# Three cross attention layers: where the head sums are fetched, normalised and projected, and where the next loads are issued

## The reference

```
def _perceiver_layer(x, inp, Wq, bq, Wk, bk, Wv, bv, Wo, bo, W1, b1, W2, b2):   # layer 1
    q = (x @ Wq + bq).reshape(b, t, NUM_HEADS, HEAD_DIM)
    k = (inp @ Wk + bk).reshape(b, s, NUM_HEADS, HEAD_DIM)
    v = (inp @ Wv + bv).reshape(b, s, NUM_HEADS, HEAD_DIM)
    attn = softmax(einsum('bthd,bshd->bhts', q, k) / sqrt(HEAD_DIM))
    out = einsum('bhts,bshd->bthd', attn, v).reshape(b, t, DIM)
    x = x + (out @ Wo + bo)
    h = gelu(x @ W1 + b1)
    return x + (h @ W2 + b2)
```

## Time and profile before

| | |
|---|---|
| median of 3 runs | 4184.68 us (4180.75 to 4191.73) |
| the profiled execution, its own time | 4188.51 us |
| span of its trace | 4186.7 us |
| PE busy | 3623.1 us (87%) |
| DVE busy | 3421.4 us (82%) |
| ACT busy | 2804.7 us (67%) |
| mean granted TensorE clock | 0.911 |

### The profile page before, as it was taken

How to read it: one execution, slowest core, us unless ns; L and a number is a source line. 1 busy time by engine, 2 the same in 40 slices (tenths; PEclk the granted TensorE clock), 3 DMA queues, 4 the chain that set the end, 5 groups by cost and what they waited for, 6 DMA issues and landing times. The chain is left out here.

```text
span 4186.7 us, 85443 instructions
## 1 busy us (share of the span) xinstructions
PE 3623.1 (87%) x35126; PEld 1223.7 (29%) x35126; DVE 3421.4 (82%) x3310; ACT 2804.7 (67%) x4037; POOL 229.1 (5%) x196
## 2 busy tenths in 40 slices
PE   5676899999999848999999997199959999999995
PEld 2352322222222212222222222045522222222221
DVE  4333899999999548999999994399969999999972
ACT  0332388888888715888888886145517888888884
POOL 3000000000000000000000000234400000000000
PEclk9657699999999967999999999599958999999998
DMA  3102011111010130111111102300011111111100
GB/s 102 48 1 55 12 28 21 22 28 27 14 28 16 53 67 13 28 28 23 19 28 28 19 11 64 73 7 6 3 30 26 26 17 28 28 21 21 28 4 22
DMA packets 56053, 117.15 MB, mean 28 GB/s; under 512 B 10930, under 2 KB 46642, under 8 KB 50418
## 3 DMA queue, kind: packets, MB, share of 16 engines
q1 hardware_dynamic: 53108, 109.79, 14.6%
q10 hardware_dynamic: 2592, 2.36, 0.2%
HBM read 84.16 MB, written 27.86 MB: 27 GB/s over the span
## 5 line engine op out<-in xcount | busy, mean ns | idle before, releaser
L1759 DVE TENSOR_REDUCE chunk_max<-max_scores 128x2 f32<-128x988 f32 (+1 forms) x2496 | 2788.2, 1178 | 126.6 <-PE max_scores L1621 87.6
L1738 ACT ACTIVATE probs<-scores 128x512 f32<-128x512 f32 (+1 forms) x3231 | 2453.0, 808 | 461.9 <-PE scores L1647 437.5
L1674 PE MATMUL values_sum<-probs,values 128*9 128x256 f32 x19584 | 1368.4, 382 | 0.0
L1647 PE MATMUL scores<-queries,key_ring 49*128 49x512 bf16 x4800 | 1227.2, 384 | 44.7 <-ACT probs L1738 12.1
L1621 PE MATMUL max_scores<-key_ring,queries 48*128 48x494 bf16 (+1 forms) x4992 | 980.8, 392 | 159.2 <-DVE chunk_max L1759 106.5
L1674 PEld LDWEIGHTS values_sum<-probs,values 128*9 128x9 f32 x19584 | 374.8, 89 | 758.6 <-issue 571.1
L1647 PEld LDWEIGHTS scores<-queries,key_ring 49*128 49x128 bf16 x4800 | 305.4, 94 | 637.0 <-ACT probs L1738 546.2
L1621 PEld LDWEIGHTS max_scores<-key_ring,queries 48*128 48x128 bf16 x4992 | 240.0, 94 | 852.5 <-DVE chunk_max L1759 530.1
L1339 ACT ACTIVATE probs<-scores 128x512 f32<-128x512 f32 x256 | 138.4, 592 | 106.2 <-PE scores L1291 106.2
L1365 DVE TENSOR_REDUCE chunk_max<-max_scores 128x1024 f32 (+1 forms) x128 | 155.0, 1214 | 24.2 <-PE max_scores L1247 24.0
L1711 ACT ACTIVATE values<-scores 128x512 f32<-128x512 f32 (+2 forms) x45 | 25.1, 564 | 210.2 <-PE scores L1631 196.4
(11 more groups left out here) (190 smaller groups left out, 1704.1 us busy)
## 6 DMA issues: line engine op xcount, KB each, us to landing
key_ring<-k_parts SPq DMA_DIRECT2D x96, 300.2 KB
key_ring<-k_parts SPq DMA_DIRECT2D x96, 200.1 KB
key_ring<-k_parts SPq DMA_DIRECT2D x96, 100.1 KB
k_parts<-queries SPq DMA_DIRECT2D x72, 128.0 KB, 2.4
o_whole<-values_sum_s SPq DMA_DIRECT2D x48, 128.0 KB, 7.8
k_parts<-k_part SPq DMA_DIRECT2D x36, 128.0 KB, 2.4
queries<-q_rows SPq DMA_DIRECT2D x6, 672.0 KB, 8.9
context<-in_ctx_t SPq DMA_DIRECT2D x1, 3202.0 KB, 17.1
```

Of the source, the lines that this page charges most:

```text
L1647: return pe.matmul(sc[:, g % 3, :], keys(rows, h, P * t, P * (t + 1)), qb[rows, q], start=True, stop=True)
L1674: mm = pe.matmul(acc[32 * b:32 * b + WV, 0:QBLOCK], vb[rows, h, t, :], pr[rows, slot, QBLOCK * (b % 2):QBLOCK * (b % 2 + 1)], start=(t == ...
L1738: act.activation(pr[:, a % RING:a % RING + b - a, :], sc[:, a % 3:a % 3 + b - a, :], ACT.Exp)\
L1759: dve.tensor_reduce(mx[:, h % 2, c, :, j], mxb[:, w % 2, :, 0:width], AX.X, ALU.max)\
```

## The change

Within `cross_attention`, SP now fetches the sums and the totals of head h-2 back from `o_whole` in the loop (`fetch_sums`, two DMAs a head, onto 8 partitions each), behind the store of head h-1. The fetches of heads 13 and 14 stand ahead of the key-term stores. DVE takes the reciprocals, the products and the bias of heads 0 to 14 (120 partitions) at the end of its own stream, and PE projects these 120 rows behind its last values product into a PSUM bank of the maximum scores.

The last head doesn't go through DRAM any more. A 128x128 matrix of zeros and ones (`tails[0]`) spreads its totals over the rows of sums by a matmul; DVE takes the reciprocal from PSUM, multiplies and adds a bias; four matmuls with zero-padded output weights (`tails[1]` to `tails[4]`, one for each block of query columns) add its part to the projection. DVE then adds bias and residual into `k.x`, inside the same phase. `cross_output`, `project_residual` for these three attentions, and the blocks of loads between are gone.

The feed-forward's weights are loaded at the start of the attention phase (`early`). The first two heads' keys of attention 1 are loaded at the end of SP's stream in attention 0 (`following`), behind the landing of all key-term stores; for this, attention 1 begins at ring slot 1 and no longer at 0. There are two more small inputs, `tails` (two DMAs in each attention) and `last_bias` (one more DMA among the first loads of the program). The phase has 10 semaphores more: 36, where there were 26.

The core of the diff:

```diff
         @block.sync
...
+            def fetch_sums(h):
+                sp.wait_ge(o_stored[h % 2], 16 * (h // 2 + 1))
+                rows = slice(HD * h, HD * (h + 1))
+                by_block = o_whole[h].rearrange("(b r) q -> r b q", b=4)
+                sp.dma_start(sums[rows, :].rearrange("r (b q) -> r b q", b=4), by_block[0:HD]).then_inc(fetched, 16)
+                sp.dma_start(totals[rows, :].rearrange("r (b q) -> r b q", b=4),
+                             by_block[HD:WV].to_broadcast([HD, 4, QBLOCK])).then_inc(fetched, 16)
+
             max_rows(0)
+            sp.dma_start(tails[:, 0, :], tails_d[0]).then_inc(tails_loaded, 16)
+            sp.dma_start(tails[:, 1:5, :], tails_d[1 + 4 * layer:5 + 4 * layer].rearrange("b p n -> p b n"))\
+              .then_inc(tails_loaded, 16)
+            for name, dst, src in early:
+                sp.dma_start(dst, src).then_inc(k.arrived[name], 16)
             for h in range(H):
...
                 if h >= 1:
                     store_values(h - 1)
+                if h >= 2:
+                    fetch_sums(h - 2)
                 if h + 1 < H:
                     max_rows(h + 1)
+            fetch_sums(H - 2)
             if ahead is not None:
                 for c in range(NCHUNK):
                     sp.wait_ge(next_low, c + 1)
                     store_key_terms(sp, ahead[2], part, c, c % 4, next_stored[c % 4])
-            store_values(H - 1)
-            for b in range(2):
-                sp.wait_ge(o_stored[b], 16 * (H // 2))
+            sp.wait_ge(fetched, 32 * (H - 1))
...
+            if following is not None:
+                for h in range(2):
+                    load_keys(k, sp, h, following, ahead[2], k.first_keys[layer + 1])
 
         @block.tensor
...
             for i in range(tiles_by[NOPS - 1], H * NTILE):
                 values(i)
+            for c in range(2):
+                pe.wait_ge(normed, c + 1)
+                pe.matmul(mxb[:, 0, c, 0:HALF], wo[0:HD * (H - 1), :], cols(sums, c)[0:HD * (H - 1)], start=True, stop=False,
+                          skip_group_check=True)
+            pe.wait_ge(tails_loaded, 32)
+            pe.wait_ge(acc_taken, H)
+            pe.matmul(mxb[:, 1, 0, 0:QBLOCK], tails[:, 0, :], acc_s[:, (H - 1) % 2, :], start=True, stop=True)\
+              .then_inc(last_total, 1)
+            pe.wait_ge(last_normed, 1)
+            for b in range(4):
+                mm = pe.matmul(mxb[:, 0, b // 2, QBLOCK * (b % 2):QBLOCK * (b % 2 + 1)], tails[:, 1 + b, :], last_out[:],
+                               start=False, stop=True, skip_group_check=True)
...
```

and on DVE, behind `next_key_terms` of the last chunk:

```diff
+            dve.wait_ge(fetched, 32 * (H - 1))
+            for c in range(2):
+                dve.reciprocal(cols(totals, c)[heads], cols(totals, c)[heads]).then_inc(inverted, 1)
...
+            dve.wait_ge(last_total, 1)
+            dve.reciprocal(last_inverse[:], mxb[:, 1, 0, 0:QBLOCK]).then_inc(last_inverted, 1)
...
+            for c in range(2):
+                dve.wait_ge(out_ready, c + 1)
+                dve.scalar_tensor_tensor(out=cols(k.x, c), in0=mxb[:, 0, c, 0:HALF], scalar=bo, in1=cols(k.x, c),
+                                         op0=ALU.add, op1=ALU.add)
```

More of the change, by code:

```diff
@@ L327, in load_everything @@
     k.w = {n: k.squares[:, i, :] for i, n in enumerate(SQUARES)}
+    k.last_bias = sb("last_bias", [P, 3])
     with ExitStack() as ctx:
@@ L1517, with cross_attention @@
 AHEAD_EVERY = 4
-def cross_attention(k, layer, base, qb, vb, k_parts, o_whole, wv, ahead=None):
+def cross_attention(k, layer, base, qb, vb, k_parts, o_whole, wv, wo, bo, bv, tails_d, early=(), ahead=None, following=None):
     nc = k.nc
@@ L1534, in cross_attention @@
         acc_s = sb("values_sum_s", [P, 2, QBLOCK])
+        sums = sb("sums", [P, N])
+        totals = sb("totals", [P, N])
+        last_inverse = sb("last_inverse", [P, QBLOCK])
+        last_out = sb("last_out", [P, QBLOCK])
+        tails = sb("tails", [P, 5, P])
+        tails_loaded = sem("tails_loaded")
         v_product = sem("v_product")
@@ L1832, in load_ffn @@
-def load_ffn(k, ctx, layer, w1_d, b1_d, w2_d):
+            heads = slice(0, HD * (H - 1))
+            dve.wait_ge(fetched, 32 * (H - 1))
+            for c in range(2):
+                dve.reciprocal(cols(totals, c)[heads], cols(totals, c)[heads]).then_inc(inverted, 1)
+            for c in range(2):
+                dve.wait_ge(inverted, c + 1)
+                scale = dve.tensor_tensor(cols(sums, c)[heads], cols(sums, c)[heads], cols(totals, c)[heads], ALU.mult)
+                scale.then_inc(normed if bv is None else scaled, 1)
+                if bv is not None:
+                    dve.wait_ge(scaled, c + 1)
+                    dve.tensor_scalar(cols(sums, c)[heads], cols(sums, c)[heads], bv[heads], None, ALU.add).then_inc(normed, 1)
@@ new lines, in _ @@
+            dve.wait_ge(last_total, 1)
+            dve.reciprocal(last_inverse[:], mxb[:, 1, 0, 0:QBLOCK]).then_inc(last_inverted, 1)
+            dve.wait_ge(last_inverted, 1)
+            scale = dve.tensor_tensor(last_out[:], acc_s[:, (H - 1) % 2, :], last_inverse[:], ALU.mult)
+            scale.then_inc(last_normed if bv is None else last_scaled, 1)
+            if bv is not None:
+                dve.wait_ge(last_scaled, 1)
+                dve.tensor_scalar(last_out[:], last_out[:], k.last_bias[:, layer:layer + 1], None, ALU.add)\
+                   .then_inc(last_normed, 1)
@@ L1838, in load_ffn @@
-    return layer, w1, b1, w2
+    loads = [(layer + "_w1", w1[:], w1_d), (layer + "_w2", w2[:], w2_d.rearrange("(g r) n -> r g n", r=P)),
+             (layer + "_b1", b1[:], b1_d)]
+    for name, _, _ in loads:
+        k.arrived[name] = k.ctx.enter_context(k.nc.semaphore(k.name("arrived_" + name)))
+    return (layer, w1, b1, w2), loads
 def ffn(k, x_in, weights, b2, gelu):
@@ L1880, in program, with attend @@
         o_t = hn
-        def attend(layer, prefix, src, w, bq, bv, ahead=None, then=lambda: None):
-            base = 1 if layer == 2 else 0
+        def attend(layer, prefix, src, w, bq, bo, bv, early=(), ahead=None):
+            base = 0 if layer == 0 else 1
             with ExitStack() as c2:
@@ L1990, in host_layout @@
     w2[0:DFF] = inp["L0_xattn_ff_w2"]
+    tails = np.zeros((13, P, P), np.float32)
+    last_bias = np.zeros((P, 3), np.float32)
+    for b in range(4):
+        tails[0, 32 * b + HD, 32 * b:32 * (b + 1)] = 1.0
+        for n, (wo, bv) in enumerate((("L1_xattn_Wo", "L1_xattn_bv"), ("L2_xattn_Wo", None), ("L3_xattn_ca_wo", "L3_xattn_ca_bv"))):
+            tails[1 + 4 * n + b, 32 * b:32 * b + HD] = (inp[wo].T if n == 1 else inp[wo])[HD * (H - 1):]
+            if bv is not None:
+                last_bias[32 * b:32 * b + HD, n] = inp[bv][HD * (H - 1):]
     turned = ("L2_xattn_Wq", "L2_xattn_Wk", "L2_xattn_Wv", "L2_xattn_Wo")
```

77 lines of the change are left out of this document (28 added, 49 removed).

## The result

The changed kernel takes 4126.85 us (median of 4 runs, 4125.28 to 4127.73) against 4187.66 us before (median of 4 runs, one more than in the table above): a ratio of 0.9856, with a 95% interval of 0.9839 to 0.9873. The forecast was 4128 us. The profiled execution took 4127.73 us with a span of 4125.9 us, 60.8 us less than that of before in both numbers.

What follows compares the result with a forecast made beforehand. DVE's score reductions set the pace inside the attentions; the chains behind them, 94.7 us, were one path. Gains of 61.4 us less 0.8, 1.9 and 1.8 gave 56.9: 4184.68 to 4128 us, 8 in 10 within 4114 to 4148.

Steps and rivals of the forecast that it cites:

- The chains behind the attentions are the path: From ACT's last copy to the work behind the projection, 94.7 us over three attentions are one path; shortening counts in full.
- The new tail, 7.8 and 7.4 us: From ACT's copy to the second residual step: 7.8 us in attentions 0 and 2, 7.4 in attention 1, without value bias.
- The end of the phase, 3.3 us: Ending an attention phase with 36 semaphores takes 3.3 us, between 2.5 and 3.5, as POOL clears one after the other.
- Nothing in the loop: The two fetches a head fit in 50.8 us of idle SP time, so they cost nothing; uncovered, 1.2 us a head.
- Key terms at most 4.1 us late, PE with 12 us to spare: At the loop's end, fetches delay the first key-term store by at most 4.1 us; PE has some 12 us to spare.
- The last bias, 0.8 us: One more load, `last_bias`, among the first loads, at whose end all engines wait, costs 0.8 us.
- The clock: PE's clock falls in gaps between matmuls: 1.9 us for attention 0's feed-forward, 1.8 us for one slow tail.
- The worst case: All three tails and attention 0's feed-forward run at the slow clock, leaving a gain of 53.3 us.
- Dearer tails: Rival: each tail and phase end takes twice 11 us, giving back 33 us, so 4161 us; chance 0.12.
- a new wait: Rival: PE waits for late key terms or normalising in attentions 0 and 1; 4147 us if 15 us late; chance 0.05.
- a slower loop: Rival: fetches hold up key loads or the row of maxima, 1.5 us a head, so 4197 us; chance 0.04.
- hidden transfers: Rival: the transfers were hidden anyway, gain near zero, 4185 us; chance 0.05, shared with a loss elsewhere eating the gain.

Runs made afterwards that it cites:

- the repeats: The changed kernel, unaltered, measured twice more: 4126.84 us and 4128.86 us, ratio 0.9859 to the kernel before both times.
- the two runs on it: Changed kernel with 36 unused semaphores more in each cross attention phase: 4134.38 us; changed kernel with clearing shared by four engines: 4114.90 us.
- eight fetches: Changed kernel with each fetch of heads 0 to 13 issued eight times: 4135.05 us; with only heads 0 to 12 repeated: 4130.29 us.

## Why the prediction was right, point by point

- *The chains behind the attentions are the path.* Right. 94.7 us became 33.2 (33.8 and 34.5 in the repeats); the forecast was 33.4 with 1.8 of slow clock booked apart.
- *The new tail, 7.8 and 7.4 us.* Measured 7.38 with bias at full clock, 8.68 in attention 1 at the lower one. The reciprocal from PSUM took 1.76 against 1.71. The sum was too long elsewhere: the totals' matmul starts 1.30 us behind the copy and not 1.51, and the hand-overs between DVE's steps take some 0.03 us each.
- *The end of the phase, 3.3 us.* 3.06 to 3.11; 3.57 in attention 0, where the wait for the weights is in it. That POOL clears one by one is shown by the two runs on it.
- *Nothing in the loop.* Right, and by a wide margin (eight fetches cost nothing there that can be told).
- *Key terms at most 4.1 us late, PE with 12 us to spare.* They start 2.4 us behind the store of head 14, where it was 0.4 before: 2.0 us later, not the 3 to 4 that were named as a sign, and nothing waits for them. With stores that start 17.1 us later still, PE loses about 6 us, so the cover is some 11 us, near the 12 of the prediction. In attention 2, without key terms, DVE does wait for the fetch, but its rows are ready at 4035.7 and PE wants them at 4074.6.
- *The last bias, 0.8 us.* Its issue takes 0.69 us; a price in the whole is not shown, since executions of one kernel differ by more.
- *The clock.* One slow tail was booked, at 1.8 us; the first profile has one, at 1.7, and the repeats have two and three, at 2.3 and 3.0 us together. Attention 1's tail is slow in all three and the others now and then; what decides it, no run shows, so the size is right and the exact hit is luck. The worst case, three slow tails at 5.4 us, did not come: the repeat with three slow tails lost 3.0. The feed-forward lost 2.9 us (2.0 in one repeat), not 1.9: the granted clock was 0.50 (1.2 GHz) when it began, as the windows above show.
- *The rivals.* Dearer tails, a new wait, a slower loop and hidden transfers did not come; the experiments show no trace of the first three in the changed kernel. On the rule of the Trainium skill for DMAs with fewer than 16 rows outermost ("DMA: Bandwidth & Descriptors", section "Rules for kernel authors") no run shows a cost, and none changed the layout of the fetches: unloaded, a pair of fetches in the run with eight of them follows the other every 2.5 us, issue and landing together.
- The sum came to 56.9 us, the profile shows 60.8. The terms that were too small or missing are the tails (by 1.9 us) and attention 1 (4 us, of which 2.8 belong to the one execution of before that was compared); the feed-forward and the end went 2 us the other way.
- The time, 4128 us, was met within 1.2 us although the gain was 3.9 us short. It was taken off the median of three runs, 4184.68, and with a fourth run that median is 4187.66; from there the same gain would have given 4130.8. So close a hit is in part luck; the mechanism and the size of the gain are not.

## What to carry to other kernels

Behind a loop whose engines are all busy, the short chain of store, fetch and small phases is a path by itself: find it in the timeline, from the last copy of the loop to the next large work, and not in shares of busy time. What can be normalised early should not wait for the last piece; that piece is worth a detour of five small matmuls. Loads for later belong where nothing is queued behind them: the same twelve key loads held up the fetch of the old tail (48.3 us with the loads ahead of it, 30.6 with them moved), and a tail that still stores its last head loses 7 us to them.

## What the runs showed of the hardware

- Clearing semaphores at the end of a phase costs about 0.07 us each on one engine, 2.55 us for 36 more; shared by four engines, all phases of this kernel together give back 12 us.
- A 128 KB store that lands in 1.7 us on an idle queue took 9.1 us with 2.4 MB of key loads issued 12 to 16 us ahead of it.
- Behind a gap of 2.3 to 2.7 us between matmuls the clock stayed at 2.4 GHz in three tails of nine and fell to 1.2 GHz within the next matmuls in six: behind all three gaps of 2.31 us, and behind three of the six of 2.70 us.
- One head of the same program lasts 61.2 to 63.6 us, in step with the moment at which the clock rises in it, in all 36 first heads on record.
